# Attention and low-rank feed-forward kernel: the column term of the zero points added to x by GpSimd instead of by TensorE, with a new order of loads, statistics and conversions

## The reference, cut to what matters

```python
def fake_quant(x, s, z):
    q = jnp.clip(jnp.round(x / s + z), 0.0, 255.0)
    return (q - z) * s
x = x + matmul(fake_quant(layernorm(x), s1, z1), fake_quant(ctx, s2, z2))      # phase 1
h = layernorm(x)                                                              # phase 2
A = einsum('bn,nri->bri', gate, lora_A); B = einsum('bn,nor->bor', gate, lora_B)
x = x + matmul(h, W) + bias + B (A h) + B_shared (A_shared h)
```

## Time and profile before

| what | value |
|---|---|
| median of 3 runs | 1062.89 us (1061.36 to 1066.37) |
| the profiled execution | 1063.74 us, of which span 1061.7 us |
| granted TensorE clock, mean | 0.989 |
| TensorE busy | 1003.1 us (94%) |
| VectorE, ScalarE, GpSimd busy | 532.3, 311.5, 163.4 us |

### The profile page before, as it was taken

One profiled execution on the slowest core, in us unless ns is written; L12 is line 12 of the kernel. 1 busy time (PEld: TensorE's weight loads), 2 busy tenths in 40 slices (PEclk: granted clock), 3 DMA queues, 4 the chain that ended last, 5 costly groups with the idle time before them and its releaser, 6 DMA issues.

```text
span 1061.7 us, 12294 instructions
## 1 busy us (share of the span) xinstructions
PE 1003.1 (94%) x4791; PEld 472.9 (45%) x4791; DVE 532.3 (50%) x764; ACT 311.5 (29%) x266; POOL 163.4 (15%) x199
## 2 busy tenths in 40 slices
PE   2778999799999999999999999999999999999996
PEld 1345444355544444444444444445544444444442
DVE  6754677879655455463423555987632023014010
ACT  4666731322032132232223743532121021003000
POOL 3101100101102211311510000020104004004110
PEclk9989999899999999999999999999999999999998
DMA  8869682767735446338599844456935025004010
GB/s 365 255 192 368 260 346 96 184 139 183 201 127 195 168 149 212 138 112 251 204 299 262 336 179 159 80 166 147 222 110 169 20 80 187 20 30 158 10 42 27
DMA packets 124392, 181.70 MB, mean 171 GB/s; under 512 B 96064, under 2 KB 96064, under 8 KB 111808
## 3 DMA queue, kind: packets, MB, share of 16 engines
q1 hardware_dynamic: 109600, 118.25, 37.3%
q0 software_dynamic: 13600, 58.73, 15.3%
q10 hardware_dynamic: 1152, 4.19, 1.0%
HBM read 128.72 MB, written 29.36 MB: 149 GB/s over the span
## 4 chain that ended last, share of the span: by engine, by line
PE 68%; DVE 11%; DMA 10%; issue 4%; ACT 3%; POOL 1%; SPq 1%; DVEq 0%; POOLq 0%; ACTq 0%
PE psum L1154 16%; PE psum L1156 16%; PE psum L1155 16%; PE psum L987 15%; DMA stage<-in_w 2%; DMA x<-in_x 2%; PE psum L1177 2%; DMA lhs<-in_lora_b 1%; DVE ring L1396 1%; DMA xn<-in_x 1%; DVE stats L1421 1%; DVE hl L1441 1%; DVE stats L1308 1%; DMA bias_sb<-in_bias 1%; DMA lhs<-ap_st 1%
## 5 line engine op out<-in xcount | busy, mean ns | idle before, releaser
L1154 PE MATMUL psum<-ring,lhs 128*128 128x512 f16 x1024 | 388.8, 380 | 9.4 <-DMA lhs<-hl 7.4
L1155 PE MATMUL psum<-ring,lhs 128*128 128x512 f16 x1024 | 388.8, 380 | 0.0
L1156 PE MATMUL psum<-ring,lhs 128*128 128x512 f16 x1024 | 388.8, 380 | 0.0
L987 PE MATMUL psum<-ring,lhs 128*128 128x512 bf16 x1024 | 235.2, 386 | 9.0 <-DMA lhs<-ap_st 7.1
L987 PEld LDWEIGHTS psum<-ring,lhs 128*128 128x128 bf16 x1024 | 101.4, 99 | 134.8 <-issue 15.4
L1154 PEld LDWEIGHTS psum<-ring,lhs 128*128 128x128 f16 x1024 | 100.3, 98 | 132.3 <-issue 10.1
L1156 PEld LDWEIGHTS psum<-ring,lhs 128*128 128x128 f16 x1024 | 100.4, 98 | 121.3 <-issue 0.8
L1155 PEld LDWEIGHTS psum<-ring,lhs 128*128 128x128 f16 x1024 | 100.3, 98 | 119.9 <-issue 0.8
L1448 DVE SCALAR_TENSOR_TENSOR x<-psum,sc,x 128x512 f32<-128x512 f32 (+1 forms) x64 | 45.3, 746 | 182.2 <-PE psum L1166 181.4
L748 ACT ACTIVATE ring<-stage,sc 128x2048 f16<-128x2048 f32 x32 | 63.7, 2002 | 202.6 <-PE psum L1156 159.4
L617 POOL TENSOR_TENSOR x<-x,bias_sb 128x512 f32<-128x512 f32 (+1 forms) x64 | 87.7, 1396 | 173.5 <-DVE xn L1431 98.2
(11 more groups left out here) (158 smaller groups left out, 644.9 us busy)
## 6 DMA issues: line engine op xcount, KB each, us to landing
stage<-in_w SPq DMA_DIRECT2D x38, 1024.0 KB, 6.0
stage<-in_ctx_in SPq DMA_DIRECT2D x30, 1024.0 KB, 7.9
out<-x POOLq DMA_DIRECT2D x64, 256.0 KB, 3.5
x<-in_x POOLq DMA_DIRECT2D x8, 1024.0 KB, 11.9
xn<-in_x POOLq DMA_DIRECT2D x8, 1024.0 KB, 7.3
x<-in_x POOLq DMA_DIRECT2D x4, 2048.0 KB, 15.9
...
```

Source lines behind the costliest of these rows:

```text
L987: last = pe.matmul(psum[:, t, :], lhs_q[:, k, t * P:(t + 1) * P], ring_q[:, g, j % 2, u, :], start=(k == 0), stop=False)
L1154: pe.matmul(psum[:, t, :], hi, ring[:, g, 0, u, :], start=(kk == 0), stop=False)
L1155: pe.matmul(psum[:, t, :], hi, ring[:, g, 1, u, :], start=False, stop=False)
L1156: last = pe.matmul(psum[:, t, :], lo, ring[:, g, 0, u, :], start=False, stop=False)
```

## The change

1. The column term. `column` now writes T0 * S12 * sum as one f32 row into `bias_sb` (the ones of the sum are 1.0 rather than 2^5). `column_low` and `column_term` are gone: the last matmul of group 3 closes the tile. GpSimd adds `bias_sb` to x, 128 x 512 f32, once a tile (`add_column`, 64 times in all), and `evict1` waits for that add.
2. GpSimd's list. The adds stand between its DMAs and its all-reduces. `largest(3)` now stands behind the first add of block 3.
3. Loads. x of tile 0 comes as four pieces on SP's queue instead of one on GpSimd's; the gate and scale parameters move to ScalarE's queue; groups 0 and 1 of ctx block 1 are loaded behind the four transposes; the LoRA B loads are drawn ahead of group 3 of ctx block 1, and ctx block 2 waits for the end of `b_effective`; two LoRA A loads go out earlier.
4. VectorE's list at the start (statistics of tile 0 ahead of the pattern, `variance` and `scale_rows` of tiles 4 and 5 earlier, `round1` of 3, 4, 5 earlier) and at the end of phase 1 (`w_group` 0 ahead of `low2` of tile 1, `stats2` of tile 2 behind `w_group` 2).
5. `base0_pair` starts with tile 0 alone, and needs the low half of tile 1 only after three groups of matmuls.

```diff
             sp.wait_ge(x_in[1], 16)
             load_ctx(0, 0, [0, 1])
-            load_ctx(0, 1, [0, 1])
             for t in range(PT, TILES):
                 turn_q(t)
+            load_ctx(0, 1, [0, 1])
...
             load_lora_b(0)
+            load_lora_b(1)
             load_ctx(0, 1, [2])
-            load_lora_b(1)
-            load_ctx(0, 1, [3])
             load_lora_b(2)
             load_lora_b(3)
+            load_ctx(0, 1, [3])
+            sp.wait_ge(be_full, 8)
             load_ctx(0, 2, [0, 1])
...
+            def add_column(b, j, tiles=range(TILES)):
+
+                pool.wait_ge(col_ready, b * NBLK + j + 1)
+                for t in tiles:
+                    if b == 0 and j == 0:
+                        pool.wait_ge(relued, t + 1)
+                    else:
+                        pool.wait_ge(with_row, (2 + j) * TILES + t + 1 if b else TILES + t + 1)
+                    v = x2[:, t, j * NW:(j + 1) * NW]
+                    pool.tensor_tensor(v, v, bias_sb[:, :], ALU.add).then_inc(with_col, 1)
...
+                add_column(b, 1)
+                store_a(b, [0, 1])
+                add_column(b, 2)
+                store_a(b, [2, 3])
+                add_column(b, 3, [0])
+                if b == 0:
+                    largest(3, MX_W, PW_W)
+                add_column(b, 3, range(1, TILES))
...
-                    act.activation(col_parts[:, n % 2, :], psum[:, CB, :], ACT.Copy, scale=D1).then_inc(col_hi, 1)
+                    if n:
+                        act.wait_ge(with_col, n * TILES)
+                    act.activation(bias_sb[:, :], psum[:, CB, :], ACT.Copy, scale=D1).then_inc(col_ready, 1)
...
-                                     start=(k == 0), stop=False)
-                if g < NG - 1 and t == TILES - 1:
+                                     start=(k == 0), stop=(k == KT - 1))
+                if g == NG - 1:
+                    last.then_inc(psum_full, 1)
+                elif t == TILES - 1:
                     last.then_inc(ring_free, 1)
...
-            def column_term(b, j, tiles):
-
-                n = b * NBLK + j
-                pe.wait_ge(col_ready, n + 1)
-                for t in tiles:
-                    pe.matmul(psum[:, t, :], ones[:, :], col_parts[:, n % 2, :], start=False, stop=True).then_inc(psum_full, 1)
...
                 def base0_pair():
 
-                    for t in range(2):
-                        tile_in(t)
-                        bank_free(k, t)
-                    for g in range(NG):
+                    tile_in(0)
+                    bank_free(k, 0)
+                    pe.wait_ge(converted, grp_w(b, 0, 0) + 1)
+                    base_group(0, 0)
+                    high_in(1)
+                    bank_free(k, 1)
+                    high_group(1, 0)
+                    pe.wait_ge(converted, grp_w(b, 0, 1) + 1)
+                    base_group(0, 1)
+                    low_in(1)
+                    low_group(1, 0)
+                    base_group(1, 1)
+                    for g in range(2, NG):
...
-                dve.wait_ge(with_row, (2 + j) * TILES + t + 1 if b else min(j, 1) * TILES + t + 1)
+                if b == 0 and j == 0:
+                    dve.wait_ge(with_row, t + 1)
+                else:
+                    dve.wait_ge(with_col, (b * NBLK + j) * TILES + t + 1)
...
                 evict1(b, j, 3)
-                early_stats2(b, 2)
-                late_stats2(b, 2)
+                w_group(b, 0, 0)
                 low2(b, 1)
                 evict1(b, j, 4)
                 evict1(b, j, 5)
-                w_group(b, 0, 0)
                 w_group(b, 0, 1)
                 evict1(b, j, 6)
                 evict1(b, j, 7)
                 w_group(b, 0, 2)
+                stats2(b, 2)
                 w_group(b, 0, 3)
```

More of the change, by code:

```diff
@@ L18 @@
 CENTRE = 127.0
-ONES = 2.0 ** 5
-COL_SCALE = 2.0 ** -16
+ONES = 1.0
 EPS = 1e-5
@@ L182, in build @@
         x_in = [sem(f"x_in{n}") for n in range(TILES)]
+        x0_in = [sem(f"x0_in{n}") for n in range(NBLK)]
         res_in = [sem(f"res_in{n}") for n in range(NBLK)]
@@ L343, in _ @@
         def _(sp):
-            sp.dma_start(pats_sb[:, 0:4 + NGATE], par).then_inc(par_in, 16)
+            for c in range(NBLK):
+                sp.dma_start(x2[:, 0, c * NW:(c + 1) * NW], x_tile[0, 0][:, c * NW:(c + 1) * NW]).then_inc(x0_in[c], 16)
             def turn_q(t):
@@ L544, in root_pair @@
                 pool.tensor_tensor(ROOT2, VEPS2, NEG_HALF, ALU.pow).then_inc(pair_root, 1)
-            load_x(range(4))
+            load_x(range(1, 4))
             pool.memset(ident, 0.0).then_inc(pats, 1)
@@ L594, in load_residual, with store_a @@
                                x_tok[b][:, :, j * NW:(j + 1) * NW]).then_inc(res_in[j], 16)
-            def store_a(b):
-                for g in range(GPB):
+            def add_column(b, j, tiles=range(TILES)):
[7 more added lines that the diff above has]
+                    pool.tensor_tensor(v, v, bias_sb[:, :], ALU.add).then_inc(with_col, 1)
+            def store_a(b, gs):
+                for g in gs:
                     pool.wait_ge(a_lo, b * (GPB + 1) + g + 2)
@@ L1034, in tile_start @@
                 bank_free(blk(b, 0, j), t)
+                if t == CB:
+                    pe.wait_ge(col_ready, b * NBLK + j + 1)
                 if b == 0 and j == 1:
@@ L1103, in first_block @@
                         group1(0, t, g)
-                    column_term(0, 0, range(t + 1) if t == PT else [t])
                 for c in range(NBLK):
@@ L1120, in first_by_tile @@
                         column_sum(b, j)
-                    first = 1 if tail else TILES // 2 - 1
-                    if t >= first:
-                        column_term(b, j, range(t + 1) if t == first else [t])
                 if tail:
@@ L1129, in first_by_tile @@
                             group1(j, t, g)
-                    column_term(b, j, range(TILES - tail, TILES))
             def base(b, t, j, k, gi):
@@ L1146, in last_bases, with high_group, low_group @@
                         base_group(t, g)
+            def high_group(t, g):
+                for u in range(GU):
+                    kk = g * GU + u
+                    hi = lhs[:, 0, kk, t * P:(t + 1) * P]
+                    pe.matmul(psum[:, t, :], hi, ring[:, g, 0, u, :], start=(kk == 0), stop=False)
+                    pe.matmul(psum[:, t, :], hi, ring[:, g, 1, u, :], start=False, stop=False)
+            def low_group(t, g):
+                for u in range(GU):
+                    lo = lhs[:, 1, g * GU + u, t * P:(t + 1) * P]
+                    pe.matmul(psum[:, t, :], lo, ring[:, g, 0, u, :], start=False, stop=False)
             def base_group(t, g):
@@ L1264, in _ @@
             then(dve.tensor_scalar(T1, Z2, -1.0, CENTRE, ALU.mult, ALU.add))
-            then(dve.tensor_scalar(D1, T0, COL_SCALE, None, ALU.mult))
+            then(dve.tensor_tensor(D1, T0, S12, ALU.mult))
             then(dve.tensor_tensor(D2S, T1, S12, ALU.mult))
@@ L1305, in stats1 @@
             def stats1(t, parts=range(NBLK)):
-                dve.wait_ge(x_in[t], 16)
+                if t:
+                    dve.wait_ge(x_in[t], 16)
                 for c in parts:
+                    if t == 0:
+                        dve.wait_ge(x0_in[c], 16)
                     last = dve.bn_stats(stats[:, t % 2, c, :], x2[:, t, c * NW:(c + 1) * NW])
@@ L1350, in row_terms @@
                 dve.tensor_scalar(RC, RSUM, D2S, KD, ALU.mult, ALU.add).then_inc(rows_ready, 1)
-            def column_low(b, j):
-                n = b * NBLK + j
-                v = col_parts[P // 2:P, n % 2, :]
-                dve.wait_ge(col_hi, n + 1)
-                dve.scalar_tensor_tensor(out=v, in0=psum[P // 2:P, CB, :], scalar=D1[P // 2:P, :], in1=v,
-                                         op0=ALU.mult, op1=ALU.subtract).then_inc(col_ready, 1)
             def ctx_group(b, j, g):
@@ L1488, in evict_and_convert @@
                 ctx_group(b, j + 1, 0)
-                column_low(b, j)
                 ctx_group(b, j + 1, 1)
@@ L1619, in product_scale @@
                 dve.wait_ge(scales, j + 1)
+            stats1(0)
+            variance([0])
             dve.wait_ge(pats, 2)
@@ L1642, in _ @@
             round1(2)
+            round1(3)
             stats1(5, range(2))
-            round1(3)
             turn_out(2)
             stats1(5, range(2, NBLK))
+            variance([4, 5])
             head_group(2)
             turn_out(3)
-            variance([4, 5])
+            scale_rows([4, 5], 3)
             head_group(3)
-            stats1(6)
-            scale_rows([4, 5], 3)
+            stats1(6, range(2))
+            round1(4)
+            stats1(6, range(2, NBLK))
+            round1(5)
             stats1(7)
             variance([6, 7])
-            round1(4)
             scale_rows([6, 7], 4)
-            round1(5)
             round1(6)
             round1(7)
-            column_low(0, 0)
```

33 lines of the change are left out of this document (18 added, 15 removed).

## The result

The changed kernel took 1092.67 us (median of 4 executions, 1087.95 to 1095.61), the kernel before 1064.25 us beside it (1061.36 to 1066.37): a ratio of 1.0265, 95% interval 1.0211 to 1.0318. It is slower by 28 us; the forecast was 1053.6. The profiled execution is the fastest of the four, 1087.95 us with a span of 1086.4 us.

The account below looks back on a forecast made before the run. TensorE bounds most stretches; elsewhere a chain through VectorE, ScalarE, GpSimd and DMAs does. Batch 0 gives 5.1 us and batch 1 4.2, together 9.3: 1063.74 becomes 1054.4, or 1053.6 for the median; range 1046 to 1063.

Parts of the forecast that it names:

- Start: Batch 0's beginning: x in pieces and a shorter VectorE list win about 1 us ahead of tiles 4 and 5.
- Row terms: Block 0, batch 0: ScalarE still starts them at 64.55; `a_effective` starts near 66, ends about 80.6; 10 us won.
- the clock at 2.15 us: Block 1's column sum, batch 0: after about 8 us idle, 16 matmuls run slower, losing 2.15 us.
- Middle: Up to block 1's column sum, batch 0: last ctx group lands at 93.5, sum at 107.2 instead of 112.72.
- Rival C: The start gives nothing, as the same bytes end at the same time; 5.5 us missing, 1059.1 us; chance 0.14.
- keeps its length: Phase 2 of batch 0: from tile 3 on TensorE has 10.4 us a tile against VectorE's 7.3, so no change.
- Swaps: GpSimd, batch 0: switching code between all-reduces and adds costs 7.3 us each, bounds 6.3 and 12.4.
- D: Rival: GpSimd's code swaps take longer, each microsecond beyond 7.3 counting four times; gain gone at 9.6 us each; chance 0.14.
- "About 1 us" of waiting: Batch 0: the column sum of block 2 waits about 1 us, behind VectorE's evictions, LoRA low parts and ctx groups.
- End of phase 1: Delayed VectorE chain makes tile 2 of phase 2 wait: loss 2.2 us in batch 0, 1.0 in batch 1.
- Batch 1: No swaps; three blocks save 1.73 us each, 5.2 us, less 1.0 at the end of phase 1: 4.2 us gained.
- Rival E: GpSimd's adds and VectorE hold each other up; an add takes 2.3 us instead of 1.27: 1059.6 us; chance 0.08.

Follow-up runs that it names:

- e5: Kernel before with only the new start: x of tile 0 in four pieces on SP's queue, parameters on ScalarE's, tile 0 statistics first; 1070.87 us, ratio 1.0042.
- e3: Changed kernel with the 16 matmuls of tile 7 of block 0 done three times, to fill TensorE's idle time; 1084.37 us, ratio 1.0183.
- e9: Kernel before with the column term on GpSimd and the middle piece of the reordering, old start and old end; 1081.95 us, ratio 1.0149.
- e4: Changed kernel with GpSimd's adds of block 0 waiting until VectorE has scaled the row sums; 1086.81 us, ratio 1.0204.
- e6: Kernel before with only the middle piece: tiles 4 and 5 rounded earlier, LoRA and ctx block 1 loads reordered; 1061.90 us, ratio 0.9959.
- e2: Kernel before with only the column term moved to GpSimd, old order otherwise; 1069.68 us, ratio 1.0048.
- e8: Kernel before with only the end-of-phase-1 piece: new order of W groups and tile 2's statistics, pair started group by group; 1074.53 us, ratio 1.0074.
- the two halves: Kernel before with only the reordering (column term on TensorE), ratio 1.0108, and with only the column term on GpSimd, ratio 1.0048.

## Why the prediction was wrong

**Start: the first failed step.** "About 1 us is won" ahead of tiles 4 and 5, from x in pieces. VectorE could take the third and fourth piece only at 10.9 and 14.0 us, and the first matmul came 6.2 us late (21.25 against 15.02). The prediction has no row for a load in pieces, and does not ask what GpSimd's queue draws beside them. By itself the start costs 5 us of time (e5).

**Row terms: the step that failed most.** "ScalarE's row terms still start at 64.55", "evictions end near 72, `a_effective` starts near 66 and ends at about 80.6". They started at 75.74: some 6 us from the start, 5.1 from VectorE held by the adds. `a_effective` started at 77.46 and ended at 105.0, and its 13.1 us more are the largest single item on the way to block 1. Behind them the fourth group of ctx block 1 was converted at 114.29, where I had its load at 93.5. I had priced the clock at 2.15 us, after the idle time that I did foresee (before the column sum), from a row with 512-column matmuls; the stage after the idle time that I did not foresee is the one of 128x64 f32 matmuls, and it never left 1.2 GHz. e3 and e9 show the item, e4 both links of it.

**Middle: right.** Alone, with the old start, it does what the steps said: `a_effective` from 66.86 (66), the fourth group of ctx converted at 94.14 (93.5), the column sum of block 1 at 108.03 (107.2) after a wait of 7.60 us (8), and still 4.5 us ahead at block 3. Rival C, that it gives nothing, falls. But e6 is only 1.2 us ahead at block 1 of batch 1, so phase 2 of batch 0 took back some 3 us of it, in this profile. I had written that phase 2 "keeps its length". Two of the 3 us are waits for VectorE: in this stretch TensorE waits 3.2 us for groups of W (before 1.6) and 2.3 for VectorE's LoRA part, `ap_st` (before 1.7).

**Swaps: right in price, D falls.** The idle times of GpSimd behind the all-reduces are 6.66 and 6.99 us, the one ahead of the third all-reduce 6.27; the one ahead of the first two is 7.93, and the profile puts its end down to ScalarE. I took 7.3, the rival 9.6 or more. The Trainium skill's figure (GPSIMD Engine Reference, Instruction dispatch, about 6 us) lies below all of them. (D's threshold had a slip: 1068.2 is 14.6 us above the forecast, 3.65 a swap, so it would be 10.95 us, not 10.6.) What I had too low is what follows the swap in block 1: four evictions in step with adds (one in 1.24 us instead of 0.66) and the low parts of LoRA, whose inputs lie in SBUF, slowed beside the adds as these rows of after and before show:

```profile
L1597 DVE SCALAR_TENSOR_TENSOR lhs<-b_st,sc,lhs 128x512 f16<-128x512 f32 x2 | 2.7, 1377 | 0.0
L1604 DVE SCALAR_TENSOR_TENSOR lhs<-lhs,sc 128x512 f16<-128x512 f32 x8 | 8.7, 1122 | 0.0
```

```profile
L1555 DVE SCALAR_TENSOR_TENSOR lhs<-b_st,sc,lhs 128x512 f16<-128x512 f32 x2 | 1.4, 746 | 0.0
L1562 DVE SCALAR_TENSOR_TENSOR lhs<-lhs,sc 128x512 f16<-128x512 f32 x8 | 5.6, 746 | 0.0
```

From the column sum of block 1 to that of block 3 the changed kernel needs 65.15 us, before 60.57; e2 needs 64.64. I had expected less than before. "About 1 us" of waiting came as 4.96 us in three waits (0.82, 2.14, 2.00) and a dip of the clock.

**End of phase 1: right in batch 0, too small in batch 1, and phase 2 did not keep its length.** I had a loss of 2.2 us in batch 0, at the start of tile 2 of phase 2, and 1.0 in batch 1. TensorE there, with its wait for the third group of W and then tile 2:

```profile
237.78 0.39 PE L1184 MATMUL psum<-ring,lhs 128*128 128x512 f16 x1 [2.55 <-DVE ring L1436]
...
254.63 0.38 PE L1184 MATMUL psum<-ring,lhs 128*128 128x512 f16 x1 [1.13 <-issue]
...
305.43 0.39 PE L1195 MATMUL psum<-b_st,ap_st 128*128 128x512 f16 x1 [3.59 <-DVE ap_st L1506]
```

From block 3's column sum to tile 2 the changed kernel takes 61.2 us, before 58.5 (173.49 to 232.03): 2.7 us. The chain on VectorE in front of it came as forecast (the low half of tile 2 ends at 250.15, within 0.5 us of 229.9 shifted to the later block 3), although its sum had a slip: 36.1 less 4.0 plus 5.2 is 37.3, not 37.7. In batch 1 the same stretch is also 2.7 us longer, and 2.3 are left at the end; that term was too small. What I had at nothing is the rest of phase 2 in batch 0: the stretch from block 3's column sum to block 1's in batch 1 is 5.9 us longer in all (436.77 against 430.85). The 3.59 us at 305.43 stand where before TensorE waited 0.24 us (at 278.23). Alone, on the kernel before, the new order loses more, 5.5 us in batch 1 and about 4 from block 3 to the next batch (e8); why the changed kernel loses less there was not settled.

**Batch 1.** From block 1 to block 3 the full 1.73 us a block are won (55.68 against 59.14 us), as forecast. Block 0 gives 1.0, as the next column sum waits 0.58 us for VectorE, and the end takes 2.3 back. From block 0's column sum on (581.68 before, 608.52 after) batch 1 thus gains 2.1 us, not 4.2.

**Rival E had the right pair of engines and the wrong victim.** It let an add grow to 2.3 us. Their median stayed at 1.27, as forecast, and a few long ones (up to 3.3 us) brought the mean to 1.54; the larger price came from VectorE. The port rule that the prediction quotes from the Trainium skill (GPSIMD Engine Reference, Specifications) names contention of this pair, not how long it lasts: it would have pointed to the place, had I asked which small VectorE instruction on the path falls into the run of adds.

**Together.** Start 5, end 8, column term 5, less 4 for the middle: 14 us, all measured alone; the two halves gave 16. The 12 us and more to the measured 28 do not come from any piece alone. e9 shows an effect of this size, 16 us, of the column term with the middle piece: the wait that had kept TensorE late was taken away, and the idle time went to the place where it costs the clock. That the changed kernel's 12 us are this same effect is concluded from the same rows in both (a hold of 5.4 us, 7.4 us of idle time, 27.5 us at 1.2 GHz); the kernel with the hold and the half clock both taken out was not run.
